# A four-layer graph network in fp32: the distance search in fp32r products grouped by format, and the last layer ordered by the arrival of gathered rows

## What is computed

```python
z = leaky_relu(_lap_mul(A, x) @ W1 + b1, 0.1)      # z: 4096 x 128
sq = sum(z * z, -1)
d2 = maximum(sq[:, None] + sq[None, :] - 2.0 * (z @ z.T), 0.0)
S = exp(-sqrt(d2 + 1e-10) / 2)
S = where(ranks < 4, S, 0.0)                        # the 4 nearest of each row
A2 = S + A
out = _lap_mul(A2, x) @ W2 + b2                     # d * (A2 @ (d * x))
```

## Time and profile before

| what | us |
|---|---|
| median of 3 runs | 1520.61 (1513.95 to 1523.7) |
| the profiled execution: its own time | 1512.57 |
| the profiled execution: span | 1510.7 |
| busy in the span: PE, DVE, ACT, POOL | 1424.8, 1210.1, 789.4, 176.1 |

### The profile page before, as it was taken

One profiled execution on the slowest core, in us unless ns is written; L12 is line 12 of the kernel. 1 busy time (PEld: TensorE's weight loads), 2 busy tenths in 40 slices (PEclk: granted clock), 3 DMA queues, 4 the chain that ended last, 5 costly groups with the idle time before them and its releaser, 6 DMA issues.

```text
span 1510.7 us, 15178 instructions
## 1 busy us (share of the span) xinstructions
PE 1424.8 (94%) x5244; PEld 886.5 (59%) x5244; DVE 1210.1 (80%) x1617; ACT 789.4 (52%) x1111; POOL 176.1 (12%) x177
## 2 busy tenths in 40 slices
PE   7999999999999999999989898999999999879993
PEld 4556677787788677777776672222222223666672
DVE  7987888889998887665589995788888888577883
ACT  2312233357666776655576653444444444576863
POOL 0000000000000000000000000000000000687886
PEclk9999999999999999999999999999999999989997
DMA  8777665568767756665587790000000003979992
GB/s 329 243 263 225 220 207 188 191 222 297 263 223 237 278 192 213 209 195 181 173 315 259 262 340 16 0 7 7 7 7 1 7 7 110 371 271 365 384 348 86
DMA packets 82859, 291.46 MB, mean 193 GB/s; under 512 B 10848, under 2 KB 10976, under 8 KB 82784
## 3 DMA queue, kind: packets, MB, share of 16 engines
q1 hardware_dynamic: 78048, 280.01, 53.9%
q0 software_dynamic: 4736, 10.49, 2.2%
HBM read 286.27 MB, written 4.19 MB: 192 GB/s over the span
## 4 chain that ended last, share of the span: by engine, by line
PE 67%; DVE 14%; POOL 11%; issue 5%; ACT 2%; DMA 1%; SPq 0%; POOLq 0%; ACTq 0%; DVEq 0%
PE ps L581 18%; POOL landing L1225 10%; PE ps L413 9%; PE ps L415 9%; PE ps L414 9%; PE ps L418 8%; DVE A_lo L1041 7%; PE ps L582 5%; PE ps L486 1%; PE ps L514 1%; PE ps L515 1%; POOL picks L1222 1%; PE ps L455 1%; DVE hn L895 1%; PE ps L449 1%
## 5 line engine op out<-in xcount | busy, mean ns | idle before, releaser
L1041 DVE TENSOR_TENSOR A_lo<-ring,A_hi 128x1024 fp32r<-128x1024 f32 x426 | 502.7, 1216 | 67.2 <-ACT A_hi L619 65.9
L619 ACT ACTIVATE A_hi<-ring 128x1024 fp32r<-128x1024 f32 x426 | 437.8, 1055 | 146.5 <-PE ps L415 120.1
L413 PE MATMUL ps<-A_hi,G_odd_hi 128*128 128x512 f32 x716 | 294.7, 412 | 30.9 <-DVE A_lo L1041 30.9
L581 PE MATMUL ps<-in_b 128*128 128x512 f32 x512 | 289.6, 648 | 4.6 <-DVE colsum L1031 4.6
L415 PE MATMUL ps<-A_hi,G_odd_lo 128*128 128x512 f32 x716 | 283.5, 396 | 0.0
L414 PE MATMUL ps<-A_lo,G_odd_hi 128*128 128x512 f32 x716 | 283.0, 395 | 0.0
L619 ACT ACTIVATE scores<-ps,neg_sq 128x2048 f32<-128x2048 f32 x64 | 126.0, 1968 | 196.2 <-PE ps L582 196.2
L1114 DVE MAX8 rows_T<-scores 128x8 f32<-128x4096 f32 x32 | 141.7, 4427 | 63.8 <-ACT scores L619 63.8
L413 PEld LDWEIGHTS ps<-A_hi,G_odd_hi 128*128 128x128 f32 x716 | 136.7, 191 | 78.0 <-issue 38.6
L1225 POOL DMA_INDIRECT landing<-scaled_rows,picks x128 | 158.3, 1237 | 39.5 <-issue 31.3
L1215 POOL DMA_DIRECT2D scaled_rows<-G_last x8 | 6.2, 780 | 1280.1 <-ACT G_last L619 1280.1
(11 more groups left out here) (132 smaller groups left out, 1209.4 us busy)
## 6 DMA issues: line engine op xcount, KB each, us to landing
ring<-adj_t SPq DMA_DIRECT2D x524, 512.0 KB, 4.7
X<-x_rows SPq DMA_DIRECT2D x8, 256.0 KB, 7.4
scaled_rows<-G_last POOLq DMA_DIRECT2D x8, 256.0 KB, 2.7
landing<-scaled_rows,picks POOLq DMA_INDIRECT x128, 5.5
out_rows<-X SPq DMA_DIRECT2D x8, 256.0 KB, 6.2
pack<-packed SPq DMA_DIRECT2D x1, 836.0 KB, 14.4
pack<-packed SPq DMA_DIRECT2D x1, 192.0 KB, 4.0
```

What stands on the lines that cost most here:

```text
L413: mm(acc, G_hi[odd][:, kb, t, :], hi, start=start, stop=False)
L581: mm(ps[:, bank_of(c), :], zt, in_b[:, c, :], start=True, stop=False)
L619: return nc.scalar.activation(out_ap, in_ap, func, **k)
L1041: v_.tensor_tensor(A_lo[:, s, :, :], ring[:, s, :, :], A_hi[:, slot_of(v), :, :].bitcast(fp32), ALU.subtract).then_inc(lower_ready, 1)
```

## The change

- Search: z is kept as z_hi (fp32r) and the rest z_lo; the fp32 product becomes three fp32r products, and in each half the four bf16 products come first, then the twelve fp32r ones. `scores0` moves to the area of A_hi, since z_lo takes its place. 
- Squares: they come from ACT's row sums (4 values for each partition), are cut into three bf16 parts as 128 x 4 values on DVE, and are turned into rows by four bf16 products with a bf16 identity; ACT moves the row out. The times of layer 3's chain are drawn together.
- Last layer: all 16 visits of block 0 are whole; similarities, degrees and operand of the last block come before the visits on ACT and DVE; the steps for a gathered tile stand at the visit that `near_due` gives for it; `send` follows them. TensorE's last transposes use four banks in turn. Eight landing buffers; no copy of the indices.

```diff
-GSLOTS = 4
+GSLOTS = 8
-    3: (("DVE", "add_out", 3.3), ("ACT", "move_out", 6.3), ("PE", "natural", 6.3), ("DVE", "lap_rows", 9.5),
-        ("PE", "z_transposes", 12.0), ("ACT", "squares", 15.3), ("ACT", "z_out", 15.3), ("PE", "square_row", 17.5),
-        ("DVE", "square_parts", 21.0)),
+    3: (("DVE", "add_out", 0.3), ("ACT", "move_out", 0.3), ("PE", "natural", 1.8), ("DVE", "lap_rows", 3.0),
+        ("PE", "z_transposes", 5.5), ("ACT", "z_out", 6.5), ("ACT", "squares", 7.0), ("DVE", "z_rest", 7.2),
+        ("DVE", "square_parts", 9.0), ("PE", "square_row", 11.0), ("ACT", "aug_out", 12.0)),
-WHOLE_BESIDE_SCANS = (*range(10), 14, 15)
+WHOLE_BESIDE_SCANS = tuple(range(UNITS))
+LAST_US, NEAR_US, NEAR_FIRST = 1.5, 6.1, 9.0
+        for t in range(NT):
+            at = min(UNITS + int((NEAR_FIRST + NEAR_US * t) / LAST_US), UNITS * NB)
+            self.near_due.setdefault(self.rows_end + at, []).append(t)
...
-                mm(ps[0:3, GB, :], halves[:, :], hTs[:, :], start=True, stop=True).then_inc(sqrow_full, 1)
+                for n in range(TPB):
+                    last = mm(ps[0:3, GB, n * P:(n + 1) * P], sq_parts[:, n, :], ident16[:, :], start=True, stop=True)
+                last.then_inc(sqrow_full, 1)
...
-            def pair_columns(t, c):
-                zt = in_b[:, t // TPB, t % TPB * P:(t % TPB + 1) * P]
-                mm(ps[:, bank_of(c), :], zt, in_b[:, c, :], start=True, stop=False)
-                return mm(ps[:, bank_of(c), :], ones3[:, :], sq_aug[:, c, :], start=False, stop=True)
+            def pair_columns(t, cs):
+                at_row = t % TPB * P
+                hi, lo = (z[:, t // TPB, at_row:at_row + P] for z in (z_hi, z_lo))
+                for c in cs:
+                    mm(ps[:, bank_of(c), :], ones3[:, :], sq_aug[:, c, :], start=True, stop=False)
+                for c in cs:
+                    mm(ps[:, bank_of(c), :], hi, z_hi[:, c, :], start=False, stop=False)
+                    mm(ps[:, bank_of(c), :], hi, z_lo[:, c, :], start=False, stop=False)
+                    last = mm(ps[:, bank_of(c), :], lo, z_hi[:, c, :], start=False, stop=True)
+                last.then_inc(half_full, 1)
...
             def z_out(b):
                 act.wait_ge(zT_full, nth_in(3, b))
-                f(in_b[:, b, :], ps[:, TB, :], ACT.Copy)
-                act.wait_ge(sqrow_full, rank[3, b])
-                f(hTs[:, :], ps[:, TB, :], ACT.Square).then_inc(z2_ready, 1)
+                f(z_hi[:, b, :], ps[:, TB, :], ACT.Copy).then_inc(zhi_ready, 1)
+            def aug_out(b):
+                act.wait_ge(sqrow_full, nth_in(3, b))
+                f(sq_aug[:, b, :], ps[0:3, GB, :], ACT.Copy).then_inc(aug_ready, 1)
...
             scale_last(m - 1)
+            similarity(m)
+            new_roots(m)
+            scale_last(m)
             for j, v in enumerate(PLAN.visits[PLAN.rows_end:]):
                 if v.split:
                     upper(v)
-                if j == 13:
-                    similarity(m)
-                    new_roots(m)
-                    scale_last(m)
...
+                for t in PLAN.near_due.get(v.n, ()):
+                    scale_neighbours(t)
...
+            def z_rest(b):
+                dve.wait_ge(zhi_ready, nth_in(3, b))
+                v_.tensor_tensor(z_lo[:, b, :], ps[:, TB, :], z_hi[:, b, :].bitcast(fp32),
+                                 ALU.subtract).then_inc(zlo_ready, 1)
             def square_parts(b):
...
+                v_.tensor_scalar(neg_sq[:, TPB * b:TPB * (b + 1)], sq_cols[:, :], -1.0, None,
+                                 ALU.mult).then_inc(negsq_ready, 1)
+                half, rest = sq_rest[:, 0, :], sq_rest[:, 1, :]
+                own.add(v_.tensor_scalar(half, sq_cols[:, :], -0.5, None, ALU.mult))
+                own.settle()
+                own.add(v_.tensor_copy(sq_parts[:, :, 0], half))
+                own.settle()
+                own.add(v_.tensor_tensor(rest, half, sq_parts[:, :, 0], ALU.subtract))
+                own.settle()
+                own.add(v_.tensor_copy(sq_parts[:, :, 1], rest))
+                own.settle()
+                v_.tensor_tensor(sq_parts[:, :, 2], rest, sq_parts[:, :, 1], ALU.subtract).then_inc(sqparts_ready, 1)
...
                 if t >= GSLOTS:
                     pool.wait_ge(weighted, t - GSLOTS + 1)
-                g.tensor_copy(picks[:, k, :], best_at[:, t, 0:TOPK]).then_inc(picks_ready, 1)
-                pool.wait_ge(picks_ready, t + 1)
                 for r in range(TOPK):
                     pool.indirect_dma_start(
                         out=landing[:, k, r, :], out_offset=None, in_=scaled_rows,
-                        in_offset=bass.IndirectOffsetOnAxis(ap=picks[:, k, r:r + 1], axis=0),
+                        in_offset=bass.IndirectOffsetOnAxis(ap=best_at[:, t, r:r + 1], axis=0),
                     ).then_inc(gathered[k], 16)
```

More of the change, by code:

```diff
@@ L210, in gnn_stack @@
                 at("G_odd_lo", [P, NB, TPB, P], r32, odd_at + 16384)]
-        scores = [at(f"scores{n}", [P, N], fp32, even + 16384 * n) for n in range(2)]
+        z_lo = at("z_lo", [P, NB, BLK], r32, even)
+        scores = [at("scores0", [P, N], fp32, hi_at), at("scores1", [P, N], fp32, even + 16384)]
         near = at("near", [P, TPB, P], fp32, even)
@@ L222, in gnn_stack @@
         in_b = at("in_b", [P, NB, BLK], fp32, b_at)
+        z_hi = at("z_hi", [P, NB, BLK], r32, b_at)
         G_first = at("G_first", [P, NB, TPB, P], fp32, b_at)
         X = sb("X", [P, NB, TPB, P])
[L225 removed]
+        A_hi = at("A_hi", [P, STAGED, UK, BLK], r32, hi_at)
         pack = sb("pack", [P, PACK])
@@ L245, in gnn_stack @@
         sq_aug = colsum[0:3, :, :].bitcast(bf16).rearrange("p t (b n) -> p (t b) n", n=BLK)
-        part_hi = sb("part_hi", [3, BLK], bf16)
-        part_mid = sb("part_mid", [3, BLK], bf16)
-        rest = sb("rest", [3, BLK])
+        sq_cols = sb("sq_cols", [P, TPB])
+        sq_parts = sb("sq_parts", [P, TPB, 3], bf16)
+        sq_rest = sb("sq_rest", [P, 2, TPB])
+        ident16 = sb("ident16", [P, P], bf16)
         ones3 = sb("ones3", [3, P], bf16)
-        halves = sb("halves", [P, 3])
         ones = sb("ones", [P, 1])
@@ L352, in _ @@
                 load_unit(v)
-                if v.feeds == (4,) and v.u == UNITS - 1 and v.b >= 2:
-                    send(v.b - 2)
-            send(NB - 2)
-            send(NB - 1)
+                for t in PLAN.near_due.get(v.n - SLOTS - 2, ()):
+                    if t % TPB == TPB - 1:
+                        send(t // TPB)
+                        sent += 1
+            for b in range(sent, NB):
+                send(b)
             sp.wait_ge(out_stored, 16 * NB)
@@ L586, in pair_rows @@
                     pe.wait_ge(half_out, 2 * i + half - 1)
-                    for c in columns[4 * half:4 * half + 4]:
-                        last = pair_columns(seek[i], c)
-                    last.then_inc(half_full, 1)
+                    pair_columns(seek[i], columns[4 * half:4 * half + 4])
             def first_pairs(cs):
@@ L594, in first_pairs @@
                     pe.wait_ge(aug_ready, nth_in(3, c))
-                    last = pair_columns(seek[0], c)
-                last.then_inc(half_full, 1)
+                    pe.wait_ge(zlo_ready, nth_in(3, c))
+                pair_columns(seek[0], cs)
             last_row = seek_blocks[-1]
@@ L762, in step @@
                     candidate(b)
+                elif name == "z_out":
+                    z_out(b)
                 else:
-                    z_out(b)
+                    aug_out(b)
             def first_rectify(b):
@@ L1155, in last_rows @@
                 dve.wait_ge(nat_full, 4 * NB + b + 1)
-                own.add(v_.tensor_tensor(wide(nat), wide(near), ps[:, TB, :], ALU.add))
+                own.add(v_.tensor_tensor(wide(nat), wide(near), ps[:, TB + b % BANKS, :], ALU.add))
                 own.settle()
@@ L1180, in _ @@
             clamp(m)
-            for j, v in enumerate(PLAN.visits[PLAN.rows_end:]):
+            new_degrees(m)
+            new_inverse(m)
+            last_rest(m)
+            for v in PLAN.visits[PLAN.rows_end:]:
                 if v.split:
                     lower(v)
-                if j == 11:
-                    new_degrees(m)
-                elif j == 13:
-                    new_inverse(m)
-                elif j == 14:
-                    last_rest(m)
-                b, j = v.b - 1, j % UNITS
-                if b >= 0:
-                    for k, at_j in enumerate((5, 8, 10, 13, 15) if b else (10, 13, 15, 15, 15)):
-                        if j == at_j and k == TPB:
-                            last_rows(b)
-                        elif j == at_j:
-                            weigh(b, k)
-            for k in range(TPB):
-                weigh(NB - 1, k)
-            last_rows(NB - 1)
+                for t in PLAN.near_due.get(v.n, ()):
+                    weigh(t)
+                    if t % TPB == TPB - 1:
```

(6 more changed lines are left out.)

77 lines of the change are left out of this document (33 added, 44 removed).

## The result

The changed kernel takes 1426.5 us (median of 4 runs, 1424.2 to 1429.6), the kernel before in the same session 1520.7: a ratio of 0.941 (95% interval 0.938 to 0.945; the two medians alone give 0.938). The profiled execution took 1424.98 us after and 1512.57 before, 87.6 less, and the spans differ by 87.5. The forecast was 1423 with a sum of 93.7.

The account below looks back on a forecast made before the run. It took layer 3's end as bound by DVE, the search by PE, the last layer by POOL's gathers. Savings 59 + 14 + 6.5 + 14.2 = 93.7 off 1512.57 gave 1419, plus half the median's 8 us: 1423, range 1410 to 1433.

Parts of the forecast that it names:

- Search: Search before the last layer: PE's tile falls from 10.96 to 7.8 us, the scan's 8.87 sets the pace; 59 us saved.
- the rival that leaves the search on PE: Search: costlier format changes or a clock falling in PE's pauses, 9.4 us a tile, 1440 us in all; chance 0.14.
- Layer 3's end: End of layer 3's product: cheaper squares take DVE from 116.4 to some 98 us, stretch 105 instead of 119; 14 us saved.
- my bound of 0: Layer 3's end: nothing saved if the chain's closer times make PE wait in its queue for late steps.
- The gap: Between layer 3's last visit and the first scan: faster columns and shorter `square_parts`; net 6.5 us saved, bounds 2 and 9.
- Last scan to first gather: Start of the last layer's gathers: earlier similarities and no index copy, 11.5 us in place of 14.6.
- Pace of the gathers: Last layer on POOL: without copies and their waits 197.4 us instead of 208.7, gathers' excess left at 38; 11 us less.
- The bound of +15: Last layer's gathers: 15 us more if gathers and A_lo meet more often.
- the 4 us that I added for the runs' median: Whole kernel: half of the 8 us by which the runs' median exceeded the profiled execution, taking 1419 to 1423.
- Stalls in the last layer: Last layer: ACT waits in its queue for gathered rows, this stage's gain is gone, 1437 us; chance 0.15.
- Better balance: Layer 3 at its bound, the store in 3 us, gathers undisturbed at the end: 1399 us; chance 0.14.
- The slower one: PE at 1.2 GHz through the whole search, 15.6 us a tile, +215 us, 1640 us; chance 0.01.

Follow-up runs that it names:

- run 1: Kernel before with only the order changed: in each half the four bf16 products first, then the four single fp32 ones; 1457.5 us, ratio 0.963.
- run 4: Changed kernel with one small edit undone at a time: four landing buffers 1428.4 us, index copies back 1436.0, old places of gathered tiles' steps 1426.4, layer 3's old times 1426.5.
- run 7: Changed kernel with every last-layer visit whole, plus 98 unused DVE operations where A_lo stood: two-input subtractions 1461.9 us, one-input MAX8 1459.9 us.
- run 5: Changed kernel with every visit of the last layer whole, so no A_hi and no A_lo there; 1459.9 us.
- run 2: Changed kernel without the grouping, each column's bf16 product again ahead of its three fp32r ones; median 1510 us, executions 1467, 1486, 1534 and 1617.
- runs 6 to 8: Changed kernel, more last-layer visits whole: nine of 16 in blocks 1 to 7, 1457.6 us; all, plus DVE operations, 1461.9 and 1459.9; seven in blocks 4 to 7, 1417.8 to 1449.7.

## Why the prediction was right, and where it was off

The time, the range and the direction held, and the three stages ended where the sum had put them: on the scans, on neither engine alone in layer 3, on POOL's gathers. That the forecast came within 3.5 us is in part luck, since misses of both signs stand in the sum.

*Search, 59 against 61.3.* PE's half came out at 3.91 for 3.88 (a bf16 product 0.24 for 0.22, the two changes of format 0.2 for 0.28), a tile at 7.82 for 7.8, and the scan sets the pace at 8.86 for 8.87. The small steps between scans were too high: they cost 290.6 - 32 x 8.86 = 7.1 us instead of 9. The thought that an exposed weight load at each change of format is the waste holds (run 1), and the rival that leaves the search on PE fell. A granted clock under 0.95 in the search, which I had named as a sign of being wrong, did show in a part of it, 0.91 from 1150 to 1187, and no scan waited for it: PE had the slack.

*Layer 3's end, 14 against 10.7 in its own stretch.* DVE's work was 97.4 us for 98. PE's was 101.9 for 98, and the stretch took 108 for 105: PE's work, which I counted 4 us too low, accounts for it, and the slack beside it was 6 us for the 7 that I left. `square_parts` fell to 1.0 us instead of 1.1 in the gap's count. The closer times for the chain, which my bound of 0 was built on, neither help nor harm (run 4).

*The gap, 6.5 against 5.3.* The lower clock was there for the first few products of its second half (903.4 to 906.1), which cost about 1.4 us at 0.42 instead of 0.227 a product, and for the four bf16 products ahead of them, another 0.85. I had counted 3.9 us for this half and it took 6.0; the four columns of the first half took 3.8.

*Last scan to first gather, 3.1 against 3.4.* It took 11.23 us for 11.5. My parts, 2.2 for the queues and 0.46 for the copy, make 2.7 and not the 3.1 of the sum. Measured, the last store is issued 2.4 us sooner after the scan (5.35 for 7.73), the first gather follows it 5.9 us later instead of 6.9, of which the copy and its wait are 0.46.

*Pace of the gathers, 11 against 5.5.* This is the term that was mis-sized. The gaps were right: 202.95 - 164.2 = 38.8 us for 128 x 0.305 = 39.0. The gathers themselves were not. I left their excess over 0.94 us at 38; it came to 43.9, with nearly the same number of A_lo between first and last gather (95 for 94). In the trace of before 44 gathers took over 1.2 us, after it 48. The step that failed is to carry a third of A_lo's time over from one trace: what an A_lo costs is set by how much of it is left when a gather begins (run 7), and without the copies they begin at other times. The profiled executions with the same 98 split visits bear it out: three with copies (before, run 1, run 4) have gathers of 158.0 to 161.9 us, six without 164.2 to 168.1. The bound of +15 covered it. Runs 5 and 7 show the cause that the prediction had taken from the rows: DVE's two-input operations.

*The sum and the median.* The sum missed by 6.1 us (93.7 against 87.6), and the 4 us that I added for the runs' median was 1.5 in fact: 6.1 up and 2.5 down, so 1426.5 instead of 1423.

*The rivals.* Stalls in the last layer didn't come: PE's last visit ended at 1396.7, 18 us before POOL's last gather, near the 20 of cover counted. Better balance didn't come either. The slower one, PE at 1.2 GHz with no pause, was given 1 chance in a hundred with "nothing in the search speaks for it"; for the kernel as changed no run contradicts that, but a low clock over a part of the search is one loop's order away (run 2), and without the grouping the same kernel took 1467 to 1617 us.

*Open.* The cause of the pause of 30 to 45 us in the last layer, which came in all profiled kernels with more whole visits and in no other, isn't shown. In each of the five traces it ends only after POOL has run into its wait for a buffer, of 9.1 to 14.5 us. Run 5 shows that SP issues loads late into free places, before PE slows, and that their transfers aren't slow; in the kernel with two inputs of run 7 it is ACT and not PE that stands. What these queues have in common is that they go on late with nothing to wait for in the profile. That would fit instructions which arrive late beside the gathers, but no run shows it, and gathers of the same pace don't disturb the later stretches. Open too is why the lower clock lasts with a busy PE.

## What to carry to other kernels

Where matmuls of two formats alternate, look at the weight load in front of each change of format; if it starts only with its matmul, group by format, which here gave some 60% of the whole gain from a few lines (run 1). When one stage's gain is limited by another engine, compute that engine's pace first: below 8.87 us a tile nothing on PE counted. Price a gather by the two-input DVE operation that it begins in, up to a whole one, and try an edit that frees DVE in more than one execution: here a theory that was right on the gathers lost 33 us to something else (run 5).

## What was not expected of the hardware

- PE busy for 195 of 195 us at a granted clock of 0.50, then at 1.00 with the same instructions (run 2); the four executions lay between 1467 and 1617 us.
- A stretch of 40 us in which PE starts one matmul in 2.8 us with no wait that the profile names, at 101 GB/s instead of 348, in run 5, and pauses like it in runs 6 to 8 (90 to 120 GB/s), in one of them with ACT standing instead of PE.
- An indirect gather on POOL takes 0.94 us, and 0.94 to 1.10 beside a DVE operation with one SBUF input. One that begins within a DVE operation with two SBUF inputs, with more than 0.38 us of it left, ends 0.81 to 0.89 us after that operation, in all 110 such cases of three traces, so it takes up to 2.0 (run 7).
